# The second attention of a four-stage network: another order of row groups, another placement of the preparation, and another first threshold

## What is computed

```python
q, k, v = x @ Wq, x @ Wk, x @ Wv          # 16 heads of 64
k, v = concat(mem_k, k), concat(mem_v, v) # 4 memory rows ahead
q, k = l2norm(q), l2norm(k)
dots = einsum('bhid,bhjd->bhij', q, k) * 10
dots = einsum('hg,bgij->bhij', W_pre_th, dots)      # heads are mixed
dots = where(causal, mask_value, dots)
vk = top_k(dots, 64)[0][..., -1:]                   # the 64th largest of each row
attn = softmax(where(dots < vk, mask_value, dots))
attn = einsum('hg,bgij->bhij', W_post_th, attn)     # heads are mixed again
out = (attn @ v) * head_scale * sigmoid(x @ Wg + bg)
return out @ Wo
```

## Time and profile before

| | us |
|---|---|
| median of three runs | 3802.3 |
| the profiled execution, its own time | 3809.85 |
| its span, first to last instruction | 3807.9 |
| second attention, first to last L1268 | 1452.1 to 3458.9 |
| VectorE busy over the span | 2420.6 (64%) |
| TensorE busy | 2924.8 (77%) |
| ScalarE busy | 1918.1 (50%) |
| GpSimd busy | 1164.0 (31%) |
| granted TensorE clock, mean | 0.862 |

### The profile page before, as it was taken

The page is one execution under the profiler, slowest core; times in us unless marked ns, Lnnn a source line. Parts: engine busy times, 40 slices in busy tenths (PEclk is TensorE's granted clock), DMA queues, the critical chain, the costliest instruction groups (busy, mean ns, idle before and its releaser), DMA issues. The chain is left out here.

```text
span 3807.9 us, 61424 instructions
## 1 busy us (share of the span) xinstructions
PE 2924.8 (77%) x19206; PEld 1687.3 (44%) x19206; DVE 2420.6 (64%) x8670; ACT 1918.1 (50%) x5320; POOL 1164.0 (31%) x3252
## 2 busy tenths in 40 slices
PE   3866668667676677888888888888888788876998
PEld 1323223223232234555555655555555555553544
DVE  3243432433324328889988898899888988994444
ACT  1221312213122137777777777778777777762221
POOL 1101001010010104545545455455454554561000
PEclk6868778677786768999999999999999999987999
DMA  2101011010110112222232122222221322221000
GB/s 79 29 7 30 7 31 28 7 31 7 30 28 7 31 47 47 37 41 33 32 50 36 28 53 38 38 37 34 49 35 26 53 38 38 38 36 38 12 17 9
DMA packets 104648, 123.03 MB, mean 32 GB/s; under 512 B 20078, under 2 KB 91782, under 8 KB 103854
## 3 DMA queue, kind: packets, MB, share of 16 engines
q1 hardware_dynamic: 104366, 119.66, 17.5%
HBM read 33.49 MB, written 13.79 MB: 12 GB/s over the span
## 5 line engine op out<-in xcount | busy, mean ns | idle before, releaser
L1116 ACT ACTIVATE junk<-xs,thr 128x420 bf16<-128x420 f32 (+12 forms) x832 | 466.3, 570 | 113.9 <-POOL thr L838 112.9
L947 PE MATMUL pm<-mixin,pre_b 128*128 128x258 f32 (+15 forms) x1088 | 381.6, 467 | 146.2 <-ACT xs L1109 117.8
L960 PE MATMUL pt<-wsc,attn 128*128 128x128 f32 x2560 | 388.4, 303 | 104.3 <-POOL wsc L821 72.0
L960 PEld LDWEIGHTS pt<-wsc,attn 128*128 128x128 f32 x2560 | 341.9, 209 | 210.2 <-POOL wsc L821 136.9
L344 DVE TENSOR_REDUCE row_max<-po 128x1 f32<-128x384 f32 (+3 forms) x374 | 222.9, 638 | 284.2 <-PE po L330 284.0
L1238 DVE MAX8 best<-left 128x8 f32<-128x420 f32 (+12 forms) x832 | 368.5, 483 | 0.0
L1080 ACT ACTIVATE dots<-pa,nrm 128x258 f32<-128x258 f32 (+3 forms) x640 | 274.5, 478 | 160.9 <-PE pa L913 158.2
L252 POOL TENSOR_TENSOR rstd<-var,powers 128x4 f32<-128x4 f32 x16 | 16.1, 1008 | 1064.5 <-DVE var L262 1064.5
L913 PE MATMUL pa<-kT,qT 64*128 64x258 f32 (+3 forms) x1280 | 298.0, 468 | 52.0 <-ACT dots L1080 49.3
L947 PEld LDWEIGHTS pm<-mixin,pre_b 128*128 128x128 f32 x1088 | 183.2, 206 | 277.8 <-issue 228.7
L1172 DVE MAX8 top<-xs 128x8 f32<-128x228 f32 (+15 forms) x512 | 220.3, 438 | 125.7 <-ACT xs L1109 123.4
(11 more groups left out here) (219 smaller groups left out, 6457.7 us busy)
## 6 DMA issues: line engine op xcount, KB each, us to landing
mixin<-dots SPq DMA_DIRECT2D x32, 258.0 KB
mixin<-dots SPq DMA_DIRECT2D x32, 242.0 KB
mixin<-dots SPq DMA_DIRECT2D x32, 226.0 KB
parts_dram<-parts SPq DMA_DIRECT2D x18, 384.0 KB, 4.4
q_stack<-parts_dram SPq DMA_DIRECT2D x108, 64.0 KB
k_stack<-parts_dram SPq DMA_DIRECT2D x108, 64.0 KB
mixin<-dots SPq DMA_DIRECT2D x32, 210.0 KB
mixin<-dots SPq DMA_DIRECT2D x32, 194.0 KB
```

The lines of the kernel that those rows point to most:

```text
L947: ins = nc.tensor.matmul(bank[:, 0:jn], pre_b[:, :], mixin[:, m % MIX_SLOTS, j0:j0 + jn], start=True, stop=not last)
L960: ins = nc.tensor.matmul(bank[:, P * k:P * k + P], attn[:, m % A_SLOTS, P * k:P * k + P], wsc[:, m % A_SLOTS], start=True, stop=True)
L1116: ins = nc.scalar.activation(junk[:, z, 0:width(n)], xs[:, m % X_SLOTS, 0:width(n)], ACT.Sign, scale=-1.0, bias=thr[:, s % LIVE, z:z + 1], ...
```

## The change

Five edits, all in the second attention:

1. `SEQ`: in tile 0 the row groups 8 to 15 come ahead of 0 to 7. What depended on the order follows: `gated_rows` and `load` by SEQ, and `renewed` decides which attention slots are cleared (four more a batch element, 0 to 3).
2. The table of preparation: squares go from steps 10 to 14 into steps 2 to 9, the input's transposes from 9 to 1, the root from 16 to 11, keys, queries and their rows into steps 13 to 22, tile 3's scores into 23 to 28, tile 1's into 1 to 6, tile 2's into 8 to 13. The input rows get a third slot.
3. A tail product only for a tile's last row group: one matmul and one smaller copy a tile in place of four matmuls and two copies.
4. The maximum of both row groups of a pair by one TENSOR_REDUCE with negation, in place of two MAX8 and a multiplication. The exact pass takes its MAX8 itself (`in_turn`).
5. No aggregation (L1180) on VectorE. GpSimd adds the means and the sums of squares of even and odd elements (`halved`), and the tables are divided by the square root of the count.

```diff
-SEQ = [PER_TILE * t + u for t in TILE_ORDER for u in range(PER_TILE)]
+SEQ = [PER_TILE * t + u for t in TILE_ORDER for half in ((0, 1) if t else (1, 0)) for u in range(PER_BLOCK * half, PER_BLOCK * (half + 1))]
+ROWS_SLOTS = 3
-            OPEN = 9 - STEPS
+            OPEN = 1 - STEPS
             for b in range(nb):
                 now, before = STEPS * b, STEPS * (b - 1)
-                for c in range(NC):
-                    put(now + c // 2, "BC"[c % 2], "qk", b, 1, c, 0)
-                    put(now + 6 + c, "B", "qk", b, 2, c, 0)
-                for k, (s, slot) in enumerate(((4, "B"), (5, "A"), (5, "B"), (5, "C"), (6, "C"))):
-                    put(now + s, slot, "vx", b, k)
+                put(before, at((1, "A")), "xT", b)
+                put(before, at((2, "B"), (3, "B"), (4, "C"), (6, "C"), (7, "C"), (8, "C"), (9, "BC")), "ns", b)
+                put(before, at((11, "A")), "root", b)
+                put(before, at((17, "BC"), (20, "C"), (22, "B")), "kt", b)
+                put(before, at((18, "C"), (19, "C"), (20, "B"), (21, "C")), "qt", b)
+                put(before, at((23, "C"), (24, "ABC"), (25, "AABC"), (26, "BC"), (27, "BBC"), (28, "ABC")), "qk3", b)
+                put(now, at((1, "BC"), (2, "CC"), (3, "C"), (4, "C"), (5, "C"), (6, "C")), "qk1", b)
+                put(now, at((4, "B"), (5, "BC"), (6, "B"), (8, "B")), "vx", b)
+                put(now, at((8, "C"), (9, "AC"), (10, "B"), (11, "B"), (12, "B"), (13, "BC")), "qk2", b)
+                put(now, at((14, "C"), (15, "BC"), (16, "BBCC"), (17, "A")), "qk0", b)
                 for o in range(TT):
-                    for z in range(2):
-                        put(now + STEPS_TILE * o + STEPS_TILE - 2 + z, "A", "g", b, o, z)
-                for c, (s, slot) in enumerate(((14, "B"), (15, "B"), (15, "C"), (16, "B"), (16, "C"), (17, "A"), (17, "B"), (17, "C"))):
-                    put(now + s, slot, "qk", b, 0, c, 0)
-                put(before + 9, "A", "xT", b)
-                for i, (s, slot) in enumerate(((10, "A"), (10, "C"), (11, "C"), (12, "A"), (12, "C"), (13, "C"), (14, "A"), (14, "C"))):
-                    put(before + s, slot, "ns", b, *divmod(i, TT))
-                put(before + 16, "A", "root", b)
-                for i, (s, slot) in enumerate(((18, "B"), (18, "C"), (19, "B"), (19, "C"))):
-                    put(before + s, slot, "qt", b, i)
-                for t, (s, slot) in enumerate(((19, "A"), (20, "A"), (21, "C"), (22, "C"))):
-                    put(before + s, slot, "kt", b, t)
-                for c, (s, slot) in enumerate(((22, "B"), (23, "B"), (23, "C"), (24, "B"), (24, "C"), (25, "A"), (25, "B"), (25, "C"))):
-                    put(before + s, slot, "qk", b, 3, c, 0)
-                for c, (s, slot) in enumerate(((26, "A"), (26, "B"), (26, "C"), (27, "A"), (27, "B"), (28, "A"), (28, "B"), (29, "A"))):
-                    put(before + s, slot, "qk", b, 3, c, 1)
-                for t, s in enumerate((17, 18, 20, 21)):
+                    put(now + STEPS_TILE * o, at((6, "C"), (7, "B")), "g", b, o)
+                    beside.setdefault(now + STEPS_TILE * o + 14, []).append(("wo", b, o))
+                for t, s in enumerate((13, 14, 18, 21)):
                     beside.setdefault(before + s, []).append(("rows", b, t))
...
+            def renewed(m):
+                k = m % SUBS
+                return k < A_SLOTS or SEQ[k] // PER_TILE != SEQ[k - A_SLOTS] // PER_TILE or width(SEQ[k]) < width(SEQ[k - A_SLOTS])
             def has_tail(s):
-                return SEQ[PAIR * s % SUBS] % PER_TILE >= PER_TILE - GROUP
+                return SEQ[PAIR * s % SUBS] % PER_TILE == PER_TILE - PAIR
...
-                load(0)
+                for b in range(min(nb, 2)):
+                    load(b)
                 for s in range(N + 2 * STEPS_BLOCK + 8):
-                    if local == 9 and b + 1 < nb:
-                        load(b + 1)
+                    if local == 10 and 0 <= b < nb - 2:
+                        load(b + 2)
...
                 def first_threshold(s):
                     pool.wait_ge(moments_done, search_nth[s])
-                    chain.link(nc.gpsimd.tensor_tensor(spreads[:, p], meanvar[:, p, :, 1], halves, ALU.pow))
+                    chain.link(nc.gpsimd.tensor_tensor(halved[:, p], moments[:, p, :, 1:3], moments[:, p, :, 4:6], ALU.add))
+                    chain.link(nc.gpsimd.tensor_tensor(spreads[:, p], halved[:, p, :, 1], halves, ALU.pow))
+                    nc.gpsimd.tensor_scalar(thr[:, p], halved[:, p, :, 0], 0.5, 1.0, ALU.mult, ALU.mult)
                     nc.gpsimd.tensor_tensor(slopes[:, p], spreads[:, p], w("slope")[:, n:n + PAIR], ALU.mult)
                     chain.link(nc.gpsimd.tensor_tensor(shift[:, p], spreads[:, p], w("first")[:, n:n + PAIR], ALU.mult))
-                    nc.gpsimd.tensor_tensor(thr[:, p], meanvar[:, p, :, 0], shift[:, p], ALU.add).then_inc(thr_ready, 1)
+                    nc.gpsimd.tensor_tensor(thr[:, p], thr[:, p], shift[:, p], ALU.add).then_inc(thr_ready, 1)
...
                 def post_tail(s):
-                    for z, m, n in pair_of(s):
+                    _, m, n = pair_of(s)[-1]
...
                 def maxima(s):
                     for z, m, n in pair_of(s):
                         dve.wait_ge(m_free, M.nth((m, last_piece(n))))
-                        found = chain.mark(nc.vector.max(out=top[:, p, z], in_=xs[:, m % X_SLOTS, 0:width(n)]))
                         if search:
-                            seen = chain.mark(nc.vector.bn_stats(moments[:, p, z], xs[:, m % X_SLOTS, 0:width(n) - GROUP * R8]))
-                    chain.after(found)
-                    nc.vector.tensor_scalar(negm[:, p], top[:, p, :, 0], -1.0, None, ALU.mult).then_inc(negm_done, 1)
+                            ins = nc.vector.bn_stats(moments[:, p, z], xs[:, m % X_SLOTS, 0:width(n) - GROUP * R8])
                     if search:
-                        chain.after(seen)
-                        for z in range(PAIR):
-                            ins = nc.vector.bn_aggr(meanvar[:, p, z], moments[:, p, z])
                         ins.then_inc(moments_done, 1)
+                    both = PAIR * s % X_SLOTS
+                    nc.vector.tensor_reduce(negm[:, p], xs[:, both:both + PAIR, 0:span(s)], X, ALU.max, negate=True).then_inc(negm_done, 1)
...
-                        if n % PER_TILE < A_SLOTS:
+                        if renewed(m):
                             nc.vector.memset(attn[:, m % A_SLOTS, wn:full_width], 0.0)
...
+        summed = sqrt(width(n) - GROUP * R8)
+        first[:, n], slope[:, n] = first[:, n] / summed, slope[:, n] / summed
```

75 lines of the change are left out of this document (42 added, 33 removed).

## The result

The changed kernel takes 3863.26 us (median of 4 runs, 3859.67 to 3867.52); the kernel before took 3806.14 us beside it. The ratio is 1.0148, 95% interval 1.0123 to 1.0172: slower by 57 us, where 170 us less was forecast.

A forecast was written before the change was run, and what follows sets the result against it. VectorE was taken to bound tile 3 only, preparation to delay the others; 80.3 + 55.5 + 61 + 36.5 = 233.3 us per element against 255.8, seven times, and 12 off the last: 3641 profiled, 3632 median, range 3560 to 3735.

The forecast's parts named there:

- tile 0's list of what stays idle: Tile 0, upper block first: 8.5 us idle added to 27.7 us of VectorE work, taken as 36.5 us.
- and leaves the narrow ones without: Tile 0: score products go beside the 100- and 132-wide pairs, none beside the narrow pairs, where 4 us stay idle.
- so it still fits: Tile 3: ScalarE, busy 63.2 us, takes 9.4 more for eight squares, 72.6 of 80.3, with less lead.
- the round trip of 1.27 us for 0.84 us of work: Preparation through two PSUM banks: one score product goes round in 1.27 us while ScalarE works 0.84 on it.
- squares half hidden: Tile 3: six squares cost 1.7 us each, 10 us per element; 3702, or 3716 with tile 2 at 63; chance 0.17.
- Slower: Tile 3: eight squares paid in series, 3.6 us each, 29 per element, less 3.0; 3857 us in all; chance 0.04.
- tile 3 over 84: Sign of being wrong: tile 3 longer than 84 us with waits for ex in it; 79 to 82 was expected.
- Tile 0 over 42: Sign of being wrong: tile 0 over 42 us with a granted clock under 0.8; 34 to 40 was expected.
- the later end of tile 1's scores: Tile 3: these scores end in step 6 instead of 3; given nothing, or 2 to 3 us per element if uncovered.
- narrow steps starve: Tile 0: without preparation beside narrow pairs TensorE's clock drops and the tile stays at 45 us; 3692 in all; chance 0.12.
- 3.0 off: Tile 3: paired maxima and no aggregates save VectorE 3.0 us, taken off the tile's length.
- more than one of them at once is left out: Range 3560 to 3735: holds the forecast and three rivals each at its own price, or GpSimd's latency uncovered, not several together.

The follow-up runs named there:

- the old table: Changed kernel with the preparation's places and the loading of rows as in the kernel before; new order, arithmetic and tail product kept: 3780.20 us, ratio 0.9917.

## Why the prediction was wrong

**Two steps failed.** The larger is tile 0's list of what stays idle, with "and leaves the narrow ones without" ahead of it: 3 us beside the values, 1.5 for the step with four products, 4 in the narrow steps, 8.5 in all. Measured in the fourth element are 23.4 us idle, and 17.1 even with the old table. The narrow steps alone have 13.6 (13.0 with the old table) instead of 4: they take 22.6 us, and TensorE is busy in 17.9 of them. So the new order did not give the 8.5 us per element that it was credited with.

The second is "so it still fits", in the paragraph on the squares. It held ScalarE's busy time, 72.6 us, against the stretch, 80.3, and let the rest be slack. Measured were 68.2 busy of 85.4 in the fourth element: ScalarE was less busy than forecast and the tile still longer. The sums of a tile hide what a single step shows. The added products and squares, without VectorE work, cost 0.4 us or less in each of four steps and 2.9 us in step 7; in the changed kernel's step 7 ScalarE's copy for VectorE stands behind such items. The forecast had the round trip of 1.27 us for 0.84 us of work, and charged it in tile 0 only.

The rival "squares half hidden" charged 1.7 us for each of the six squares in tile 3, 10 us. The run with eight pairs of products and squares added shows 10.7 in the median, but 6.2 at the higher clock, so the agreement is partly luck. "Slower" gave 3857 against 3863 measured, and that is luck as well: its place, tile 3, grew by 10.5 and not by 26 us, and the rest came from tiles 0 and 1. Of the signs of being wrong, "tile 3 over 84" came true, though the waits in it are for xs and not for ex. "Tile 0 over 42" did too, but at a clock of 0.86 and not under 0.8. TensorE's waits for mixin stayed short.

**Tile 3**, 80.3 forecast, 87.0 measured. VectorE's terms (7.1 for six reductions, 3.0 saved) were right: busy 80.0. The error is idle time, 5.4 of 85.4 us in the fourth element, 2.9 of them in step 7, and the lower clock in steps 2 and 3 of some elements: tile 3 is 85.4 us where the clock is 0.98 in it and 88.5 where it is 0.94. To the later end of tile 1's scores, which makes three items in slot C of step 6, the forecast gave "nothing"; moving those scores and the values alone costs tile 3 5.8 us.

**Tile 1**, 55.5 against 62.4. Without the squares it is 54.7, so that term was right. What came in their place, scores of tiles 2 and 0, was left out of the sum; put into the old table they cost tile 1 5.5 us, and the gates 1.1. There they meet the squares, which the changed kernel has moved away, so how its 7.7 us over 54.7 divide is not shown.

**Tile 2**, 61 against 62.9, inside the 59 to 63 that were named.

**Tile 0**, 36.5 against 50.1, the largest error, 13.6 us per element. Of these 7.4 are there with the old table too (43.9): gates, projection and the wide mixing of the next element stand in the narrow steps in either table, and the sum had 4 us of idle time for them. The other 6.2 come with the new table, and its places for tile 3's scores alone give them (50.6). The values with step 28 were put at about 3 us idle; step 28 alone had 10.9 - 3.3 = 7.6. The gates make step 31 long but not the tile (49.6 without them). The rival "narrow steps starve" (45) named the place; its reason, the clock, is a part only: with the old table the four narrow steps have a granted clock of 0.96 and take 22.3 us all the same. The Trainium skill ("TensorE: Matmul & The Clock Gate", Why this matters for your kernels) has idle gaps between bursts of matmuls bring the lower clock. The changed kernel's fourth element agrees: TensorE stands idle for 1.6 us up to 2475.0 and for 1.9 up to 2480.0, and its granted clock is 0.50 from 2476.9 to 2483.7 us. The last section has a case that such gaps alone don't explain.

**The last element**, 213 against 228.7. The old table gives 216.2, so the arithmetic and the order were sized about right there (12 forecast, 9 measured), and the table costs 12.5 even without a following element. Moved alone, tile 1's scores with the values make the last element 226.8, the gates 225.2, the scores of tiles 2 and 0 221.8.

**The arithmetic** did what was said: 456 elements took

```profile
2347.25 0.61 DVE L1184 TENSOR_REDUCE negm<-xs 128x2 f32<-128x456 f32 x1
...
2347.77 0.59 DVE L1232 TENSOR_SCALAR left<-xs,thr 128x196 f32<-128x196 f32 x2
```

0.61 us long and 0.52 from its start to the next, against 0.53 forecast. VectorE's busy time per element fell by 9.7 as said. But "3.0 off" in tile 3 was taken as time because VectorE was 99% busy; measured 76.1 against 76.5. GpSimd's added work cost nothing that shows: ScalarE's longest kind of wait for thr fell from 112.9 to 45.0 us in all (80.3 with the old table). **The tail product** was set at 0 to 2.4 us per element and taken as 0; alone it measured 13 us in all, 1.6 per element. **The order** was worth nothing with the old table; with the new one it is worth 22 to 30 us.

Sum: per element 6.7 + 6.9 + 1.9 + 13.6 = 29.1 us too few, seven times, 204, and 16 in the last element; 3641 + 220 = 3861, the profiled execution. The range ended at 3735 since "more than one of them at once is left out", and the shortfalls of tiles 3, 1 and 0 came together.

## What to carry to other kernels

Where preparation passes from one in-order engine to another through a few banks, its price depends on what stands behind it in the same step. The same products and squares cost 0.4 us or less in some steps here and 2.9 in another, so compare step by step and not the busy time of a tile with its length. A low busy share of the engine in between is no proof of slack. A stretch where VectorE is 99% busy can have steps in which another engine is as late: taking 2.5 us off VectorE gave 0.4. Look at every repetition of a stretch with its clock before taking a median: 86.7 us stood between 82 at the higher clock and 89 at the lower. Take a hand-made table apart line by line before believing in it: here the arithmetic and the tail were worth 31 us and the table took back 83.
